# Expert layers of a four-layer network: chunk 0's gate and up products ahead of the router

## What is computed

```
logits = x @ gate_w;  probs = softmax(logits)          # 8 experts
top_w, top_i = top_k(probs, 2);  top_w /= sum(top_w)
combine = sum_k top_w[k] * onehot(top_i[k])
h = silu(x @ w_gate[e]) * (x @ w_up[e])                # every expert, 176 wide
moe_out = sum_e combine[e] * (h_e @ w_down[e])
sh = silu(x @ sw_gate) * (x @ sw_up)                   # shared expert, 352 (L0) or 704 (L3) wide
out = moe_out + (sh @ sw_down) * sigmoid(x @ shared_gate_w)
```

## Time and profile before

| | us |
|---|---|
| median of 3 runs | 1380.36 (1378.04 to 1382.36) |
| the profiled execution | 1380.08 |
| its span, first to last instruction | 1378.3 |
| TensorE busy | 1143.8 (83%) |
| VectorE busy | 976.2 (71%) |
| ScalarE busy | 611.9 (44%) |
| GpSimd busy | 535.9 (39%) |
| mean granted TensorE clock | 0.942 of full |

### The profile page before, as it was taken

The page is one execution under the profiler, slowest core; times in us unless marked ns, Lnnn a source line. Parts: engine busy times, 40 slices in busy tenths (PEclk is TensorE's granted clock), DMA queues, the critical chain, the costliest instruction groups (busy, mean ns, idle before and its releaser), DMA issues. The chain is left out here.

```text
span 1378.3 us, 16687 instructions
## 1 busy us (share of the span) xinstructions
PE 1143.8 (83%) x5770; PEld 824.8 (60%) x5770; DVE 976.2 (71%) x1977; ACT 611.9 (44%) x1423; POOL 535.9 (39%) x440
## 2 busy tenths in 40 slices
PE   0179899999979888999599957999999966189997
PEld 0045556555557765333388846888888842068876
DVE  7868988888758996944533536888888868954354
ACT  2156666666655545345154424333333326033333
POOL 4437767676503221530064323444444410405520
PEclk9999999999989999999699978999999988579999
DMA  2032122121011102200543421111010000011101
GB/s 93 12 88 56 38 50 62 39 63 26 21 33 46 39 24 82 102 0 1 204 153 135 174 73 56 32 32 32 32 31 31 5 8 31 0 48 46 46 28 61
DMA packets 31091, 73.41 MB, mean 53 GB/s; under 512 B 5362, under 2 KB 15091, under 8 KB 28192
## 3 DMA queue, kind: packets, MB, share of 16 engines
q1 hardware_dynamic: 28432, 67.44, 15.8%
q0 software_dynamic: 1536, 3.86, 0.9%
q10 hardware_dynamic: 1040, 1.05, 0.2%
HBM read 55.89 MB, written 6.29 MB: 45 GB/s over the span
## 5 line engine op out<-in xcount | busy, mean ns | idle before, releaser
L175 POOL TENSOR_TENSOR sums<-scans 128x512 f32<-128x512 f32 x64 | 88.2, 1378 | 314.1 <-ACT terms L169 173.0
L531 ACT ACTIVATE probs<-ps_s,stats 128x256 f32<-128x256 f32 (+1 forms) x256 | 104.3, 419 | 58.9 <-DVE stats L621 57.5
L722 PE MATMUL ps_p<-xin,wkvq 128*128 128x512 f32 x148 | 74.0, 624 | 67.6 <-DVE xin L238 65.3
L195 DVE RECIPROCAL sums<-sums 128x256 f32<-128x256 f32 x64 | 112.1, 1752 | 2.0
L478 POOL TENSOR_TENSOR probs<-probs,stats 128x512 f32<-128x512 f32 x64 | 67.4, 1053 | 118.6 <-DVE stats L627 118.6
L621 DVE CUSTOM_DVE_ANT_0 ps_s<-ps_s,mask 128x256 f32<-128x256 f32 (+1 forms) x256 | 82.9, 383 | 8.9 <-PE ps_s L746 8.7
L180 POOL TENSOR_TENSOR sums<-sums,terms 128x512 f32<-128x512 f32 x64 | 85.5, 1336 | 5.0
L722 PEld LDWEIGHTS ps_p<-xin,wkvq 128*128 128x128 f32 x148 | 26.5, 199 | 88.5 <-issue 84.8
L920 POOL TENSOR_TENSOR L3hid<-L3hid,L3sig 128x1024 f32<-128x1024 f32 x17 | 46.1, 2719 | 75.4 <-DVE L3hid L1046 37.8
L1888 PE MATMUL K_ps_kvp<-K_wqkv_hi,K_xin_hi 128*128 128x256 f32 x256 | 75.4, 294 | 0.0
L1793 ACT ACTIVATE K_ks<-K_ps_kvp 128x256 f32<-128x256 f32 x64 | 24.6, 385 | 110.9 <-PE K_ps_kvp L1888 110.9
(11 more groups left out here) (393 smaller groups left out, 3449.9 us busy)
## 6 DMA issues: line engine op xcount, KB each, us to landing
E_fc<-l_fc_dram SPq DMA_DIRECT2D x16, 1024.0 KB, 7.2
qswap<-qraw SPq DMA_DIRECT2D x60, 128.0 KB, 2.3
K_wqkv<-l_wqkv_dram SPq DMA_DIRECT2D x16, 384.0 KB, 3.2
L3wgu<-L_w_dram SPq DMA_DIRECT2D x17, 256.0 KB, 2.6
L0wgu<-L_w_dram SPq DMA_DIRECT2D x14, 256.0 KB, 2.6
L3wdn<-L_w_dram SPq DMA_DIRECT2D x17, 128.0 KB, 2.1
wkvq<-w_l0a_dram SPq DMA_DIRECT2D x4, 512.0 KB, 4.2
wo<-w_l0a_dram SPq DMA_DIRECT2D x4, 512.0 KB, 3.7
```

The source lines that it names most:

```text
L175: pstep.mark(pool.tensor_tensor(sums[:, k, :, :], scans[:, k, :, 0, :], scans[:, k, :, 1, :], ALU.add))
L195: dstep.mark(dve.reciprocal(den, den))
L531: ins = act.activation(dst[:, i % 2, :], src[:, i % 2, :], ACT.Exp, bias=stats[:, g % 4, 4 + i:5 + i], scale=-1.0, accum_out=stats[:, g % ...
L722: ins = pe.matmul(ps[:, :], w[:, k, :], xin[:, k, h * HALF:(h + 1) * HALF], start=(k == 0), stop=(k == CH - 1))
```

## The change

The router stands behind `gate_up(0)` on TensorE, and its steps stand behind chunk 0's second multiplication (and, in L0, behind the scans of the first piece) on VectorE and behind chunk 0's second SiLU on ScalarE. `rows()` and its copy move back by one chunk, behind chunk 2. SyncE and GpSimd keep their order. Nothing is added to or taken from what is computed.

```
 ScalarE
-                route_act(act, lt, l // 6 * 2 + 1)
-                after(act, "router_done", 1)
-                ... sigmoid into wide[:, 1] ...
                 for ch in range(NCH):
                     for h in range(2):
...
-                        if (ch, h) == (1, 1):
+                        if (ch, h) == (0, 1):
+                            route_act(act, lt, l // 6 * 2 + 1)
+                            after(act, "router_done", 1)
+                            ... sigmoid into wide[:, 1] ...
+                        if (ch, h) == (2, 1):
                             after(act, "rows_done", 1)
 VectorE
-                after(dve, "router_done", 1)
-                ... the router's steps ...
                 scan_steps(0, (0,))
+                def routing():
+                    ... the router's steps, unchanged ...
                 for ch in range(NCH):
...
+                        if (ch, h) == (0, 1):
+                            routing()
 TensorE
-                ... router's 16 matmuls, first of all ...
                 for ch in range(NCH):
                     gate_up(ch)
-                    if ch == 1:
+                    if ch == 0:
+                        router()
+                    if ch == 2:
                         rows()
```

More of the change, by code:

```diff
@@ L1030, in _ @@
[L1030 to L1035, removed]
@@ L1036, in _ @@
-                dve.tensor_tensor(wide[:, 0, :, :].rearrange("p t (e i) -> p (t e) i", e=NE), w16[0], w16[1],
-                                  ALU.add).then_inc(s["comb_ready"], 1)
-                scan_steps(0, (0,))
+                scan_steps(0, (0,))
+                def routing():
+                    after(dve, "router_done", 1)
+                    after(dve, "ld_gate", 32)
+                    logits = ps_y[:, 0, 0, 0:8 * (NE + 1)].rearrange("p (t e) -> p t e", t=8)
+                    dstep.link(dve.tensor_copy(lt[:, 0, :, :], logits[:, :, 0:NE]))
+                    route_dve(dve, lt, one, rank[:, :, :], l // 6 * 2 + 1)
+                    bc = lambda v: v.unsqueeze(2).to_broadcast([P, 8, NE])
+                    dstep.link(dve.tensor_tensor(one[:, 2, :], one[:, 0, :], one[:, 1, :], ALU.add))
+                    dstep.link(dve.reciprocal(one[:, 2, :], one[:, 2, :]))
+                    for k in range(2):
+                        dstep.link(dve.tensor_tensor(one[:, 4 + k, :], one[:, k, :], one[:, 2, :], ALU.mult))
+                        dstep.link(dve.tensor_tensor(lt[:, 2 + k, :, :], lt[:, 2 + k, :, :], bc(one[:, 4 + k, :]), ALU.mult))
+                    w16 = [lt[:, 2 + k, :, :].rearrange("p t e -> p (t e)").unsqueeze(2).to_broadcast([P, 8 * NE, P // NE])
+                           for k in range(2)]
+                    dve.tensor_tensor(wide[:, 0, :, :].rearrange("p t (e i) -> p (t e) i", e=NE), w16[0], w16[1],
+                                      ALU.add).then_inc(s["comb_ready"], 1)
@@ L1084, in _, with router @@
             def _(pe):
-                after(pe, "ld_gate", 32)
-                pe.wait_ge(xin_ready, 2 * l + 2)
-                for t in range(8):
-                    for k in range(CH):
-                        ins = pe.matmul(ps_y[:, 0, 0, t * (NE + 1):(t + 1) * (NE + 1)], xin[:, k, t * P:(t + 1) * P],
-                                        wgate[:, k, :], start=(k == 0), stop=(k == CH - 1))
-                ins.then_inc(s["router_done"], 1)
+                def router():
+                    after(pe, "ld_gate", 32)
+                    pe.wait_ge(xin_ready, 2 * l + 2)
+                    for t in range(8):
+                        for k in range(CH):
+                            ins = pe.matmul(ps_y[:, 0, 0, t * (NE + 1):(t + 1) * (NE + 1)], xin[:, k, t * P:(t + 1) * P],
+                                            wgate[:, k, :], start=(k == 0), stop=(k == CH - 1))
+                    ins.then_inc(s["router_done"], 1)
                 def gate_up(ch):
```

12 lines of the change are left out of this document (3 added, 9 removed).

## The result

| | before | after |
|---|---|---|
| median of 13 runs each, us | 1380.44 (1378.04 to 1382.36) | 1385.54 (1383.08 to 1387.0) |
| ratio, 95% interval | | 1.0036 [1.0028, 1.0044] |
| the profiled execution's span, us | 1378.3 | 1381.3 |
| L0, from its first conditioning instruction to the next block's, us | 149.8 | 153.9 |
| L3, from the same to its first output DMA, us | 160.1 | 161.4 |

The account below looks back on a forecast made before the run. VectorE was taken to bound L0's loop and TensorE L3's, so delays at each entry decide. L0's 1.1 + 2.2 + 1.6 = 4.9 and L3's 1.5 gave 6.4 on 1380.08, so 1386.5 us; range 1381.5 to 1390.

Parts of the forecast that it names:

- Start of chunk 0: TensorE, both layers: chunk 0 can't start before `xin_lo` is stored and handed over, +2.6 us from the router's old start.
- Chunk 0 starts at the low clock and takes 7.75: TensorE: chunk 0 again starts slow at 1.2 GHz and takes 7.75 us (7.0 to 8.9), done at +10.35.
- The router halves, 3.5: TensorE behind chunk 0: router at full clock takes 3.5 us instead of 6.97, logits read at +14.0 instead of +7.0.
- The chain and rows, +1.1 in L0: L0's entry: later router chain, then rows behind chunk 2, bring the first weighting to +32.05 against +30.98, +1.1 us.
- GpSimd's delay, +2.2: L0, VectorE: router's steps wait for GpSimd's three operations of the first piece, +2.2 us (bounds 0 and 3.67).
- The clock in L0, +1.6: L0, TensorE: after the long wait chunk 2 starts at slow clock, +1.6 us (bounds 0 and 1.6 twice).
- L3, +1.5, no clock cost: L3: chunk 4 starts at +35.7 against +34.2, +1.5 us, with nothing charged for the clock.
- Rival B: The clock costs in L3 too, 1.6 us more, 1388.1 (0.10); or a slow router, 1393 (0.03).
- Rigid loops: Behind the first weighting (L0) and chunk 4's start (L3), saturated loops and later blocks shift as a whole.
- Table loads, at nothing: ScalarE: two more table loads in L0, in time in which it waits anyway, charged at nothing.
- Rival A: Only the chain counts, no GpSimd delay or clock loss: 1.1 + 1.5 = 2.6, 1382.7 us; chance 0.22.
- Rival C: Not slower: rows aren't the last thing L0's first weighting waits for, so it runs 2.1 us earlier; 1379.5; chance 0.08.

Follow-up runs that it names:

- e1: Changed kernel, but in L0 the last two scans of the first piece stand behind chunk 1's second multiplication on VectorE; 1381.95 us, ratio 1.0020.
- e4: Changed kernel with 12 extra matmuls of 512 columns behind chunk 1 in L0, their result read by nobody; 1384.22 us, ratio 1.0033.
- e12: The change in L3 only, L0 keeping the order of the kernel before; ratio 1.0014 to before, +1.9 us.
- e2: Changed kernel with rows and their copy back behind chunk 1, the router still behind chunk 0; ratio 1.0014 to before, +1.9 us.
- e7: Changed kernel with L0's last two first-piece scans behind chunk 1 and rows and their copy back behind chunk 1; ratio 1.0004 to before.

## Where the prediction was right and where not

L0's path to the mark in stretches, in us:

| stretch | before | predicted | after | e1 | e4 |
|---|---|---|---|---|---|
| start to logits read | 7.00 | 14.0 | 13.84 | 14.19 | 14.44 |
| router's steps, to the end of `wide` | 7.23 | 7.2 + 2.2 | 8.93 | 7.21 | 8.95 |
| to the start of the waiting chunk | 1.61 | 1.4 | 1.34 | 1.35 | 1.34 |
| that chunk, to the transposes | 5.57 | 5.57 + 1.6 | 7.08 | 5.54 | 5.53 |
| transposes to first weighting | 9.57 | 3.9 | 3.92 | 3.92 | 3.92 |
| mark | 30.98 | 35.9 | 35.11 | 32.21 | 34.18 |

- **Start of chunk 0** +2.6: +2.61 and +2.70 in the changed kernel's first profile. Right, but the reason given was incomplete (last section).
- **Chunk 0 starts at the low clock and takes 7.75:** 7.56 (L0) and 7.75 (L3: 1221.24 to 1228.99), 0.50 at 399.1 to 402.7. Right.
- **The router halves, 3.5:** 3.63, at a granted clock of 1.00. Logits at +13.84 and +14.12 for +14.0. This was the central term, and the row used for it (16 wider matmuls in 1.95) was the right one. Its division was not: 1.95 / 16 is 0.122, which would give 3.9, and the 0.11 in its place has no working. Measured is 0.113 a matmul. So the 0.1 us that this term is off owes something to luck.
- **The chain and rows, +1.1 in L0:** +1.23 in e1, where nothing else is left of the change. Right. In the changed kernel itself it is 0.92 (4.13, less 1.70 for GpSimd and 1.51 for the clock). The wait moved to where it was said: rows' copy ahead of the weighting, 1.49.
- **GpSimd's delay, +2.2:** right in kind and place, mis-sized: 1.70 (0.67 on L838 and 1.02 on L842). Three things made it less. L838 began 0.45 us into L175. L175 itself took 1.27 and not 1.59. And L177 met only the exponential and steps with one input (L840, L841), which took 0.22 and 0.20 as before. The Trainium skill, page "SBUF — State Buffer", section "SBUF: two separate sides", says that of a GpSimd instruction and a VectorE operation with two inputs in this memory, the one that starts first holds the shared ports for its whole length. This trace agrees for the two router steps that met GpSimd: both ended 0.08 behind its operation. So a lock costs only what the two have in common in time; the upper bound of 3.67, all three operations in full, was far off, and the 2.2 was a guess below it. One input isn't always safe, though: L192, a step with one input, takes 0.77 at 435.02, where L175 runs beside it, and 0.29 alone.
- **The clock in L0, +1.6:** 7.08 less 5.53 is 1.55. Right; e4 shows that it is the idle time ahead of the chunk that costs it. The way to the 1.6 was looser than the result: 9 matmuls begun where full clock gives 14 is a third lost, 1.1 us, and not half of 3.1; half is what a clock of 0.50 costs, and the slow stretch was again some 3.1 us long (420.52 to about 423.65). Also the router was followed by a low clock that cost nothing, as assumed. The wait was 3.12, not the 3.9 given, by the smaller delay and the slightly earlier logits.
- **L3, +1.5, no clock cost:** +1.55 (wait 1.44, clock 1.00 behind it); e12 and e2 put it on the rows. Rival B's extra 1.6 did not come.
- **Rigid loops:** held, 64.49 of 64.68 us busy in L0's loop, 70.97 of 71.00 on TensorE from L3's chunk 4 on. Behind the loops it didn't hold in every execution (e1, above).
- **Table loads, at nothing:** right, though the count was not: L0's entry has 8 instead of 7, one more and not two.
- **Sum 6.4:** marks +5.7, measured +5.0 and, a second time, +7.2. Of the 0.7 between 6.4 and the marks GpSimd's term is 0.5 and the chain 0.2; the rest of the miss is within what one measurement differs from the next. Right for its reasons. 5.7 lies in both intervals ([3.9, 6.1] and [5.4, 9.0]), 6.4 in the second only.

Rival A (chain alone, 1382.7) is not what the changed kernel does, but it is what e1 does (1.0020, +2.8), where GpSimd is out of the way. Rival C fell with the wait of 1.49 for the rows. The change did what it says.

## What to carry to other kernels

When a late step is moved behind an early one, look at everything that hangs behind its chain as a queue: here the late router alone cost 0.14%, the late rows alone nothing that could be measured, and both together 0.36 to 0.52%, because the second lengthens just the path that the first had used up. Cheaper than moving the whole chain is to look at its last step and ask who needs it first: one step of 1.22 us, put behind the work that the other engine waits for, gave 1.5 to 2 us in two layers together. And a side task's release (here four scans that set GpSimd going) belongs to the order as much as the task itself.

## What the runs showed of the hardware

- **A run of small matmuls doesn't hold the clock.** TensorE is busy for 3.40 of 3.40 us with the router at 1.00, and the clock is 0.50 in the stretch that follows, in both layers of every kernel with the late router (0.50 at 410.5 to 413.0 here). Before, the same instructions ran through 6.97 us at 0.50. Busy time alone doesn't tell what the clock will be.
- **A filled wait keeps it.** 3.12 us idle ahead of a chunk: 7.08 us for it. With 2.88 us of it filled by matmuls of 512 columns: 5.53. Waits of 1.44, 1.56 and 1.81: 1.00 behind all three. The extra matmuls are themselves harmless when they end ahead of the data.
- **A wait of 2.6 us can go either way.** The products with `w_down` in L0 begin with a wait of 2.59 to 2.63 us in the seven kernels compared for it. Behind 2.63 the clock was 0.50 before, and 0.52 in e7 (2.61, 500.5 to 503.5); behind 2.60 it was 1.00 in the changed kernel (504.2 to 507.2), and behind 2.59 in e1 (500.3 to 503.3). So the one row that the prediction leant on showed one of two outcomes; its wait of 3.9, and the 3.12 and 3.16 that came, are longer, and the clock fell behind both.
- **Chunk 0 now shows the landing of its weights.** ScalarE's `xin_hi` stands behind `wgu_hi`, which waits for the DMA of `L0wgu`. In the changed kernel and, below it, in e2 (ScalarE's row, then TensorE's first matmul in e2):

```profile
396.04 0.63 ACT L937 ACTIVATE L0wgu_hi<-L0wgu 128x512 fp32r<-128x512 f32 x1 [1.67 <-DMA L0wgu<-L_w_dram]
```

```profile
397.56 0.63 ACT L937 ACTIVATE L0wgu_hi<-L0wgu 128x512 fp32r<-128x512 f32 x1 [2.51 <-DMA L0wgu<-L_w_dram]
...
400.54 0.77 PE L1108 MATMUL L0ps_g<-L0xin_hi,L0wgu_hi 128*128 128x512 f32 x1 [8.52 <-DVE L0xin_lo L1021]
```

  Over the kernels with the late router chunk 0 starts at +2.61 to +3.52 in L0 and the logits follow at +13.84 to +14.75; with the early router they are at +6.7 to +7.0, since the router needs none of these weights. The time of chunk 0's weights, which the early router hid, is part of what the change gave up, some 0 to 0.9 us by execution, and the prediction didn't price it.
- **A single span says little at this scale.** Blocks without a changed instruction differed by 1.0 and 1.6 us between the two profiled executions, as much as some of the effects here. Marks of the changed kernel counted from a layer's own start differed by 0.75 (L0) and 0.28 (L3) from one profile to the other, and counted from the reading of the logits by 0.04 and 0.02.
